# Running each FFN inside the attention of its own layer, four steps behind, in a two-layer transformer kernel on one Trainium2 core

## The reference

```python
x = x + attn_a(layernorm(x))      # 16 heads of 8, causal; 3 heads reweighted by token region
x = x + ffn(layernorm(x))
x = x + attn_b(layernorm(x))      # 16 heads of 8, rotary, not causal
x = x + ffn(layernorm(x))         # the same weights again
# ffn: 128 -> 512 -> 512 -> 512 -> 128
h = silu((x @ w1.T) * s1) * ((x @ w2.T) * s2)
h = gelu((h @ h1.T) * s3);  h = gelu((h @ h2.T) * s4);  y = (h @ w3.T) * s5
```

## Time and profile before

| | us |
|---|---|
| median of 3 runs | 2515.53 (2514.89 to 2515.76) |
| the profiled execution, its own time | 2512.21 |
| its span, first to last instruction | 2510.5 |
| PE, DVE, ACT, POOL busy in the span | 2132.8, 1729.4, 1482.9, 982.5 |
| mean granted TensorE clock | 0.914 of full speed |

### The profile page before, as it was taken

One profiled execution on the slowest core, in us unless ns is written; L12 is line 12 of the kernel. 1 busy time (PEld: TensorE's weight loads), 2 busy tenths in 40 slices (PEclk: granted clock), 3 DMA queues, 4 the chain that ended last, 5 costly groups with the idle time before them and its releaser, 6 DMA issues. The chain is left out here.

```text
span 2510.5 us, 37314 instructions
## 1 busy us (share of the span) xinstructions
PE 2132.8 (85%) x13378; PEld 978.4 (39%) x13378; DVE 1729.4 (69%) x2590; ACT 1482.9 (59%) x2980; POOL 982.5 (39%) x1184
## 2 busy tenths in 40 slices
PE   0889999898996899999379889989998885999998
PEld 0323333233331677777112222222222211777776
DVE  5766777677670666665189899989989833667663
ACT  0265656666663556655127777777777772665655
POOL 2344555454542344554323232323323200544544
PEclk8688988889895899999659999999999986999999
DMA  6243534334331000000323423443343300000000
GB/s 172 64 99 66 114 69 93 85 79 103 66 66 20 1 1 1 1 1 1 75 51 66 104 64 66 88 89 66 67 104 67 66 15 10 8 10 14 13 10 17
DMA packets 99853, 136.48 MB, mean 54 GB/s; under 512 B 20560, under 2 KB 81488, under 8 KB 93520
## 3 DMA queue, kind: packets, MB, share of 16 engines
q1 hardware_dynamic: 99664, 134.02, 24.5%
HBM read 67.91 MB, written 55.57 MB: 49 GB/s over the span
## 5 line engine op out<-in xcount | busy, mean ns | idle before, releaser
L576 DVE TENSOR_REDUCE b_negmax<-ps_max 128x2 f32<-128x1024 f32 x512 | 611.5, 1219 | 97.5 <-PE ps_max L693 95.4
L660 ACT ACTIVATE b_prob<-ps_score 128x512 f32<-128x512 f32 x1024 | 547.7, 598 | 206.8 <-PE ps_score L679 205.6
L660 ACT ACTIVATE a_prob<-ps_score 128x512 f32<-128x512 f32 (+3 forms) x1024 | 384.5, 437 | 259.4 <-PE ps_score L679 256.8
L576 DVE TENSOR_REDUCE a_negmax<-ps_max 128x2 f32<-128x256 f32 (+3 forms) x512 | 410.9, 821 | 178.8 <-PE ps_max L697 173.6
L679 PE MATMUL ps_score<-b_stack_q,stack_k 50*128 50x512 bf16 x1024 | 263.5, 396 | 54.6 <-ACT b_prob L660 46.1
L714 PE MATMUL ps_out<-b_prob,b_v_aug 128*9 128x512 f32 x2048 | 277.7, 615 | 18.3 <-ACT b_o_raw L633 12.5
L493 POOL TENSOR_SCALAR_AFFINE_SELECT a_prob<-a_prob 128x512 f32<-128x512 f32 x256 | 162.5, 635 | 320.9 <-ACT a_prob L660 320.7
L974 PE MATMUL ps_score<-fb_h,w_hi 128*128 128x512 f32 x1024 | 251.9, 401 | 29.8 <-DVE fb_h L888 28.8
L974 PE MATMUL ps_score<-fa_h,w_hi 128*128 128x512 f32 x1024 | 251.5, 400 | 29.7 <-DVE fa_h L888 28.7
L693 PE MATMUL ps_max<-stack_k,b_stack_q 48*128 48x512 bf16 x1024 | 233.5, 396 | 40.6 <-issue 23.8
L679 PE MATMUL ps_score<-a_stack_q,stack_k 50*128 50x512 bf16 (+3 forms) x1024 | 202.2, 330 | 37.5 <-DMA a_stack_q<-a_nm_rows 30.6
(11 more groups left out here) (139 smaller groups left out, 2961.1 us busy)
## 6 DMA issues: line engine op xcount, KB each, us to landing
stack_k<-d_stack SPq DMA_DIRECT2D x64, 384.0 KB, 5.9
d_stack<-a_parts SPq DMA_DIRECT2D x64, 192.0 KB, 4.1
a_stack_q<-d_stack SPq DMA_DIRECT2D x32, 384.0 KB, 5.5
d_stack<-b_parts SPq DMA_DIRECT2D x64, 192.0 KB, 3.7
b_stack_q<-d_stack SPq DMA_DIRECT2D x32, 384.0 KB, 5.5
d_stack<-a_parts SPq DMA_DIRECT2D x64, 128.0 KB, 3.6
d_stack<-b_parts SPq DMA_DIRECT2D x64, 128.0 KB, 3.4
d_stack<-a_parts SPq DMA_DIRECT2D x64, 64.0 KB, 3.7
```

What stands on the lines that cost most here:

```text
L576: dve.tensor_reduce(m["negmax"][:, t, :, p], dve_banks("max", k)[:, :, 0:keys], AX.X, ALU.max, negate=True).then_inc(s["max"], 1)
L660: act.activation(m["prob"][u % PROBS][:, g, lo:S], act_bank("score", 4 * u + g)[:, 0:S - lo], ACT.Exp).then_inc(s["prob"], 1)
```

## The change

The two `ffn` stages are gone. `layer` replaces `attention`: its step n also runs the FFN of batch n-4, in the same 16 units, and has B + 5 = 21 steps. The projection moves from lag 4 to lag 3 (unit 12), the FFN's normalisation follows it in units 13 to 15, and the FFN's own parts stand as below.

More of the change, by code:

```diff
@@ L61, in wait, with first_max @@
 def wait(eng, sem, value):
-    if isinstance(value, int) and value <= 0:
+    if value <= 0:
         return
     eng.wait_ge(sem, value)
[L68 to L74, removed]
+def first_max(u):
+    blocks = sum(HIDDEN_MAXES for at in HIDDEN_UNIT.values() if at < u)
+    return u + sum(1 for v in SECOND_MAX if v < u) + blocks
 def program(nc, a, out):
@@ L119, in program @@
         setup(nc, ctx, sem, m, a)
[L120 to L123, removed]
+        for stage in (lambda sem: layer(nc, sem, m, a, "a", True, None),
+                      lambda sem: layer(nc, sem, m, a, "b", False, out)):
             own = []
@@ L183, in norm_stats @@
     for t in range(T):
[L184 to L200, removed]
+        last = dve.bn_aggr(m[of + "mv"][:, t], m[of + "stats"][:, t])
@@ new lines, in norm_stats, with norm_rstd, norm_apply @@
+    last.then_inc(s[of + "mv"], 1)
+def norm_rstd(pool, m, s, b, of):
+    pool.wait_ge(s[of + "mv"], b + 1)
+    pool.tensor_scalar(m[of + "var"][:], m[of + "mv"][:, :, 1], EPS, None, ALU.add).then_inc(s[of + "var"], 1)
+    pool.wait_ge(s[of + "var"], b + 1)
+    wait(pool, s[of + "xhat"], b)
+    pool.tensor_tensor(m[of + "rstd"][:], m[of + "var"][:], m["half"][:], ALU.pow).then_inc(s[of + "rstd"], 1)
+def norm_apply(eng, m, s, b, of):
+    eng.wait_ge(s[of + "rstd"], b + 1)
+    wait(eng, s[of + "xT_ps"], b)
@@ L201, in norm_apply @@
     for t in range(T):
[L202 to L207, removed]
+        last = eng.tensor_scalar(m[of + "xhat"][:, t, :], m["x"][:, b, t, :], m[of + "mv"][:, t, 0:1],
+                                 m[of + "rstd"][:, t:t + 1], ALU.subtract, ALU.mult)
+    last.then_inc(s[of + "xhat"], 1)
@@ L412, in _ @@
                     store_reciprocals(n - 3)
+                if out is not None and on(n, FFN + 1):
+                    send(n - FFN - 1)
                 if on(n, 0):
-                    load(n, "stack_q", "stored_q", 0)
                     store(n, "stored_k", 1)
@@ L504, in _ @@
                 pool.wait_ge(s["ones"], 2)
+            norm_rstd(pool, m, s, 0, "")
+            if rotary:
+                norm_apply(pool, m, s, 0, "")
             for n in range(STEPS):
@@ L565, in turn @@
+                dve.scalar_tensor_tensor(out=m["turned"][:], in0=banks[:, 1],
                                          scalar=m["bias_col"][:, 2 + i:3 + i], in1=m["rope"][:, 2 * i + 1],
@@ new lines, in _ @@
+                    if u == 4 and on(n, 3):
+                        dve.wait_ge(s["den"], count(16, n - 3, 16))
+                        wait(dve, s["rden_out"], count(16, n - 3))
+                        dve.reciprocal(m["rden"][:], m["den"][:]).then_inc(s["rden"], 1)
+                    if u == SLOT["nm0"] - 1 and on(n, -1):
+                        norm_stats(dve, m, s, n + 1, "")
+                    if u == SLOT["nm0"] + 1 and causal and on(n, -1):
+                        norm_apply(dve, m, s, n + 1, "")
@@ new lines, in _ @@
+                    if u == SLOT["proj"] + 3 and causal and on(n, 3):
+                        norm_apply(dve, m, s, n - 3, "f_")
+                    if u in SECOND_MAX and on(n, 1):
+                        max_of(n - 1, first_max(u) + 1)
+                    if u in GATE_UNIT and on(n, FFN):
+                        gate(b, GATE_UNIT.index(u))
+                    if u in HIDDEN_UNIT.values() and on(n, 1):
+                        for i in range(HIDDEN_MAXES):
+                            max_of(n - 1, first_max(u + 1) - HIDDEN_MAXES + i)
```

726 lines of the change are left out of this document (347 added, 379 removed).

## The result

The changed kernel takes 3125.62 us in the median of four runs, against 2515.65 for the one before on the same chip: 1.242 times as long, 95% interval 1.239 to 1.244. The forecast was 2870, with a range to 3000. The direction was right, the size 256 us short.

The account below looks back on a forecast made before the run. Attention was taken as a serial loop through PE and ACT, the FFN as PE bound. Layers of 1357 and 1438 us sum to 2795, plus 24 x 3 for the clock = 2867; predicted 2870, range 2600 to 3000.

Parts of the forecast that it names:

- 161 and 6 for the clock: Merged causal step 78 us plus rotary step 83, with 3 us a step added for the clock.
- Rival A: Hand-offs overlap, each unit takes its busiest engine's time: 132 us for two steps, 2450 in all; chance 0.12.
- the places of the waits: ACT idle before gate 2's Tanh, POOL before k's parts, PE before maxima or gates and about 2.5 us after each block.
- I take 3: Clock allowance of 3 us a step for PE's waits in units 3 to 5 and the block's start; at most 7.
- C: Clock stays low through units 0 to 6 and into both blocks, 10 us a step instead of 3: 3040; chance 0.08.
- D: Each ACT table change costs as much again as its load, emptying the pipeline, 82 us over 32 steps: 2950; chance 0.06.
- ramps and tails: Steps at each layer's start and end: first four steps 204 and 216 us, with bunched maxima at 6 and 16.
- B: q's store lands before k needs its parts, 6.3 and 2.9 us less a step, 110 in all: 2760; chance 0.15.
- Some edits cost nothing.: PROBS 4 to 2, STACKS 3 to 2, the result's store and POOL's `norm_apply` all fit in existing waits or idle time.

Follow-up runs that it names:

- c3: Changed kernel with POOL's gate low parts first, two part buffers in both layers, k and v later, fillers, three probability buffers, weighing two units behind: 2755.94 us.
- e5: Changed kernel with ten filler matmuls of 512 columns before the second scores of units 8 and 13: 3006.45 us, 119 less.
- e4: Changed kernel with Gelu replaced by Tanh in the middle layers, so one ACT table serves (output changes): 2950.93 us, 175 less.
- e10: Changed kernel with the maxima spread, two in 14 units and one in each block instead of four: 3064.39 us, 61 less.
- e2: Changed kernel with two part buffers in the causal layer, so k's parts don't wait for q's store: 3012.95 us, 113 less.
- e11: Kernel before the change with PROBS cut from 4 to 2: 2971.07 us, 452 more.
- e12: Attention alone in the new order, two maxima every unit, with four probability buffers and weighing two units behind: 1984.32 us, 59 less than with two buffers.
- e13: Changed kernel with three probability buffers and the weighing two units behind, both layers: 3152.25 us, 27 more.
- e15: e12 with xT in unit 3 and q, q turned, k, k turned, v in units 4 to 8, one product a unit: 2057.98 us, 74 more.

## Why the prediction was right, and where it fell short

**Right: the direction, and why.** The change pays if two steps take under 137 us. The prediction laid a step along PE's order, found it in series, and said 161 and 6 for the clock. Rival A (each unit as short as its busiest engine, 132) is far off: c3, with the long waits gone, is at 151.8. What leaves so little to win is PE itself. PE is busy 40.7 + 21.6 and 44.3 + 21.6 in the separate steps, 128 us for a batch that took 140. By busy time a merged pair of steps could gain 12. That is not a strict bound, since busy time holds uncovered latency and, in the causal step, a clock of 0.88: the prediction's own count for the rotary step, about 36 + 21.6, leaves 15 of 72.2. But c3's 139.0, about 130 without its fillers, shows that the merged order covered no more of that latency than the separate stages did.

**Right: the places of the waits.** POOL before k's parts, ACT before Tanh of gate 2 (6.44), PE behind it (4.11), PE before unit 4's maximum, PE about 2.2 us behind each block. Units 0 to 7 of the rotary step were put at 36.9 and took 38.7.

**Wrong: the clock, in size and in most of its places.** The step that failed is "I take 3" a step, put into units 3 to 5 and the start of the block, with units 8 to 15 walked at full clock. In units 3 to 5 the clock was low indeed (gate 2's matmuls take 2.08, and 0.81 is the mean of units 0 to 7 in the causal step). But it was low behind both blocks too, 0.76 and 0.79 in the rotary step. That step missed by 12.4 us before the allowance: 1.8 in units 0 to 7, 2.2 in the two blocks (2.37 us a quarter, not 2.08), 4.4 in units 8 to 12, 4.0 in units 13 to 15. The walk had the stand of PE behind each block, priced it as a wait, and didn't ask what it does to the matmuls that follow. e5 gave 119 us back by filling it, e4 175 by shortening it. The two blocks' 2.2 are a price that was low: eight matmuls between maxima hold PE for 2.05, not 1.86. Over 12 full steps the miss is about 121 us in the rotary layer and 37 in the causal one above what the prediction had with its 3. e5's 119 say how much of the whole miss the stands behind the blocks explain by the clock: under half.

**Rivals C and D.** Both were right in part and neither as written. C had the low clock in units 0 to 6 and in the blocks; it is low in units 0 to 7 (0.81 causal, 0.91 rotary), at 1.00 in the blocks, and low behind them. Its 3040 is the nearest of all figures to 3126, by another route. D had ACT emptying its pipeline at each change. The row has the load 0.02 us behind the copy and the Exp 0.01 behind the load: 1.28 us and no more. The Trainium skill's page "ScalarE: Activation LUTs", section "What ACT_TABLE_LOAD costs", gives 2.66 for a switch with its drain; this trace doesn't agree. Its advice in "Table sets: the hidden batching unit", to batch activations by set, is borne out in kind all the same: e4, which needs one set only, saves 175 us, through PE's clock; with the stands filled, in c3, the same edit is worth 4.

**Wrong in size: ramps and tails.** Cut where unit 0 of steps 4 and 16 begins, the first four steps took about 239 and 229 us instead of 204 and 216, the tails 235 and 256 instead of 217 and 226. That is about 97 of the miss, with 158 of the full steps 255 together. e10, which unbunches the maxima, gave 61 back, mostly outside the causal layer's full steps; the ramp was priced at 6 and 16 for it.

**B.** Its text has 6.3 and 2.9 a step; the 6.3 is the causal step's by its walk: without the store gate 2 ends near 19.4 there (the rotary 23, less 2.0 for the earlier start, 0.86 for a product and 0.75 for an operation of DVE) and not at 25.6. e2 took the store away there and gained 6.4. The size is right in part by luck, since the clock came back too and the walk had no clock in it.

**"Some edits cost nothing."** For two probability buffers this held roughly, and only with the weighing one unit behind: e11 shows 452 us for the number alone; more buffers with the weighing two behind saved 59 in attention alone (e12), nothing in e13, and at most c3's 85. The prediction's ground (an Exp waits for the weighing two units back, which ends 0.1 us after the unit starts) is the very point on which the two orders differ.

**Where the hoped-for gain went.** The FFN's matmuls weren't hidden: without them the kernel is 914 us shorter, more than the 800 of the FFN's own stages. And attention alone in the new order costs 332 us more, maxima spread evenly. Of those 332, e12 takes 59 (buffers). For the rest e15's rows point to PE's order in a unit: products and the rows of maxima stand where no wait is left to absorb them. No run gives PE the old order back, and none has three stacks again, so this is argued and not shown. How the 273 divide, and why the clock fell in e13, stays open.

## What to carry to other kernels

Before merging two stages, add up the bounding engine's busy time in both: here PE was busy 128 of 140 us, and every wait that a merged order brings comes off what is left. Price a stand of PE twice, as its length and as the slow matmuls behind it; where it can't be removed, a few idle matmuls in it can pay. A small piece of work costs little where its engine waits anyway and its full price just behind that wait, so place it before the wait, and look at the lag between producer and consumer before cutting buffers.

## What was not expected of the hardware

One stand of some 2 us straight after 9.4 us of dense matmuls at 1.00 is followed by weighings of 1.90 us instead of 1.05 and scores of 0.61 instead of 0.39 a pair: dense work just before it does not keep the clock up. And adding 20 matmuls a step made the kernel 119 us faster, with the mean granted clock at 0.905 instead of 0.853.
